# The address that an empty record reads in a gather: row 0 for all, or one row for each partition

## The reference, cut to what matters

```
support  = einsum(layernorm(x), W_weight) + W_bias         # 6250 x 256
messages = support[dst] * edge_weight[:, None]
x        = x + segment_sum(messages, src, 6250)
x        = x + lstm_part(layernorm(x))                      # 50 steps for 125 segments
```

## Time and profile before

| | us |
|---|---|
| median of 3 runs | 1850.2 |
| lowest, highest | 1849.69, 1853.89 |
| the profiled execution's own time | 1853.58 |
| its span | 1851.8 |
| busy: TensorE, VectorE, GpSimd, ScalarE | 1388.0, 1365.8, 1204.2, 543.2 |
| mean granted TensorE clock (share of full speed) | 0.885 |

### The profile page before, as it was taken

One profiled execution on the slowest core, in us unless ns is written; L12 is line 12 of the kernel. 1 busy time (PEld: TensorE's weight loads), 2 busy tenths in 40 slices (PEclk: granted clock), 3 DMA queues, 4 the chain that ended last, 5 costly groups with the idle time before them and its releaser, 6 DMA issues.

```text
span 1851.8 us, 34357 instructions
## 1 busy us (share of the span) xinstructions
PE 1388.0 (75%) x8625; PEld 1154.8 (62%) x8625; DVE 1365.8 (74%) x4146; ACT 543.2 (29%) x1869; POOL 1204.2 (65%) x1275
## 2 busy tenths in 40 slices
PE   5587744554555458998988888889889878999991
PEld 2345533443444333787777777777777668899991
DVE  7979778888888955677777777777777644566665
ACT  1112200000000000333333333333333346666660
POOL 0304867777777757777777777777777700477772
PEclk9778967777777775899999999999999999999995
DMA  8101343333333643444444444444444763333334
GB/s 210 26 23 35 50 137 76 79 79 74 80 79 74 77 61 106 128 137 141 144 138 138 139 137 139 139 136 139 138 137 137 109 124 114 113 113 112 113 101 139
DMA packets 77430, 202.26 MB, mean 109 GB/s; under 512 B 28529, under 2 KB 30790, under 8 KB 76392
## 3 DMA queue, kind: packets, MB, share of 16 engines
q0 software_dynamic: 53808, 116.85, 27.3%
q1 hardware_dynamic: 23584, 84.98, 14.2%
HBM read 160.49 MB, written 41.10 MB: 109 GB/s over the span
## 4 chain that ended last, share of the span: by engine, by line
PE 27%; POOL 24%; DVE 22%; issue 17%; DVEq 3%; DMA 3%; ACT 3%; SPq 0%; POOLq 0%; ACTq 0%
POOL big_a L522 22%; PE bank L1565 10%; DVE big_a L975 7%; PE bank L1485 5%; PE bank L1539 5%; PE bank L1514 4%; PE bank L1558 1%; DVEq L1049 1%; DVE big_c L1166 1%; ACT big_c L669 1%; DVE big_c L1171 1%; DVE listed L914 1%; ACT bank L662 1%; DVE stats L893 1%; PE bank L1433 1%
## 5 line engine op out<-in xcount | busy, mean ns | idle before, releaser
L522 POOL DMA_INDIRECT big_a<-support_scratch,stg_g x636 | 608.3, 956 | 207.0 <-issue 192.3
L1539 PE MATMUL bank<-big_a,big_c 128*125 128x256 f32 x1272 | 412.3, 416 | 92.0 <-issue 51.0
L1565 PE MATMUL bank<-big_c 128*128 128x125 f32 x3648 | 457.2, 277 | 26.9 <-DVE big_c L1171 23.8
L1565 PEld LDWEIGHTS bank<-big_c 128*128 128x128 f32 x3648 | 446.7, 192 | 48.7 <-issue 36.0
L1046 DVE TENSOR_TENSOR big_b<-big_b,bank 125x256 f32 x881 | 366.5, 416 | 132.0 <-PE bank L1539 82.9
L1040 DVE TENSOR_SCALAR big_c<-consts_sb,listed 128x125 f32<-128x125 f32 x881 | 318.8, 362 | 73.4 <-PE bank L1539 62.1
L1539 PEld LDWEIGHTS bank<-big_a,big_c 128*125 128x125 f32 x1272 | 202.7, 197 | 179.2 <-DVE big_c L1040 113.1
L492 POOL DMA_INDIRECT big_a<-support_scratch,stg_g x245 | 236.2, 964 | 82.2 <-issue 69.2
L1485 PE MATMUL bank<-big_a 125*128 125x192 bf16 x800 | 119.5, 332 | 214.1 <-DVE big_a L975 214.1
L1485 PEld LDWEIGHTS bank<-big_a 125*128 125x128 bf16 x800 | 100.4, 132 | 237.5 <-DVE big_a L975 229.4
L1558 PEld LDWEIGHTS bank<-xt,w_ih 128*128 128x128 f32 x1600 | 213.3, 195 | 13.8 <-ACT xt L578 1.9
(11 more groups left out here) (226 smaller groups left out, 1658.4 us busy)
## 6 DMA issues: line engine op xcount, KB each, us to landing
pr<-gate_input_scratch SPq DMA_DIRECT2D x64, 508.0 KB, 3.4
gate_input_scratch<-pr SPq DMA_DIRECT2D x50, 508.0 KB
big_a<-support_scratch,stg_g POOLq DMA_INDIRECT x881, 2.8
out<-big_a SPq DMA_DIRECT2D x5, 1120.0 KB
support_scratch<-pr SPq DMA_DIRECT2D x12, 448.0 KB
big_b<-in_x SPq DMA_DIRECT2D x2, 1904.0 KB
big_b<-in_x SPq DMA_DIRECT2D x1, 1792.0 KB
w_ih<-in_w_ih SPq DMA_DIRECT2D x1, 1024.0 KB
```

What stands on the lines that cost most here:

```text
L522: pool.indirect_dma_start(out=ring[:, s, :], out_offset=None, in_=sup_d, in_offset=bass.IndirectOffsetOnAxis(ap=stg_g[:, q, n:n + 1], axis ...
L1539: mm(bank[4 + s % PSR][0:SEGS, 0:D], oneh[:, s % HOTS, 0:SEGS], ring[:, s, :], start=True, stop=True).then_inc(prod, 1)
L1565: return mm(bank[b + x][:, c * SEGS:(c + 1) * SEGS], w_hh[:, k, g:g + P], h_s[:, q, k, :], start=False, stop=True, skip_group_check=True)
```

## The change

It adds one [128, 1] constant, `own_row`: the partition's number times 48 (N // P), so 0, 48, ..., 6096. In `unpack`, the cast of the unpacked rows to floats is replaced by two operations. The first writes `own_row` where the weight is zero and 0 elsewhere; the second takes the larger of that and the unpacked row. Empty records so read row 48 p in partition p. Descriptors, bytes and the destination of every gather are as they were.

```
+        own_row = sb("row_of_empty_records", [P, 1])
...
             link(V.tensor_scalar(block_no[:, 0:1], sums[:, 0:1], -1.0, float(P - 1), ALU.mult, ALU.add))
             split = float(PORTIONS[0])
+            V.tensor_scalar(own_row[:], block_no[:, 0:1], float(N // P), None, ALU.mult)
...
                 link(V.tensor_scalar(pack_i[:, 0:T], pack_i[:, 0:T], 7, None, ALU.arith_shift_right))
-                V.tensor_copy(row_of[:, a:a + T], pack_i[:, 0:T]).then_inc(unpacked, 1)
+                link(V.tensor_scalar(row_of[:, a:a + T], w_of[:, a:a + T], 0.0, own_row[:], ALU.is_equal, ALU.mult))
+                V.tensor_tensor(row_of[:, a:a + T], row_of[:, a:a + T], pack_i[:, 0:T], ALU.max).then_inc(unpacked, 1)
```

## The result

The changed kernel takes 1840.1 us (median of six runs, 1837.8 to 1843.8), the kernel before 1851.2 (six runs, 1849.7 to 1853.9). The ratio is 0.9934, with a 95% interval of 0.9922 to 0.9946: faster by 0.5 to 0.8%. The profiled execution took 1841.3 us (span 1839.5), against 1853.6 (1851.8): 12.3 us less.

The account below looks back on a forecast made before the run. GpSimd's gather issue paces portion two; in its tail, empty tiles all reading row 0 back up the DMA engines. Tail -14.9 plus operations +1.7 gives -13.2 us, from 1850.2 to 1837.0; own range 1833 to 1841, whole range 1832 to 1843.

Parts of the forecast that it names:

- The tail of portion two: Last, wholly empty tiles of portion two: with own rows no DMA backlog forms, saving 19.40 - 4.46 = 14.94 us.
- the last half's 4.46 us: End of portion two: the last half's final copy comes 4.46 us after its last gather's start, as in steady halves.
- The own rows: Gathers of empty tiles: reading 128 different rows costs the DMA engines 0.48 us a tile, like steady gathers.
- the lower of the two ends: DMA price of an own-row tile: 0.48 us from steady gathers, chosen over 1.60 us from same-row gathers.
- The first two rivals: Empty-tile gathers: own rows still cost 1.60 us (1851.9 us, chance 0.06), or between 1.256 and 1.60 (1844.4, chance 0.06).
- the one that made the kernel slower: Portion two's tail: 128 distant rows cost more than 1.60 us a tile; 1868.7 us at 2.2; chance 0.03.
- Portion one: Empty tiles ending portion one: their gather backlog hides under other work, such as VectorE's 14.10 us periods; saving nothing.
- Padding in filled tiles: 5216 empty slots in 822 filled tiles: taken as 0, at most 5.7 us; rival of more gain, 1831.3 us, chance 0.05.
- The added operations: Compare and maximum replacing the cast in unpack: 1.18 us in portion two plus 0.55 in portion one, 1.7 us lost.
- The maximum: Second added operation in unpack: 0.82 us for portion two's 636 columns, 0.40 for portion one's 245.
- The compare: First added operation in unpack: 0.81 us in portion two and 0.40 in portion one, scaled from a two-scalar operation.
- keeping the last halves near 20 us: Portion two's end, sign of a wrong prediction: gathers land early but TensorE or VectorE alone keeps last halves near 20 us.

Follow-up runs that it names:

- e3: Kernel before, with compare, maximum and own rows only in portion two's last 60 columns; ratio 1.0005 on a chip where the kernel before takes about 2380 us.
- e5: The kernel of e3 run again, against the kernel before, which took 2381.7 us on that chip; ratio 1.0009.
- e9: Shortened program ending when portion two is added, without recurrence or what follows; added operations kept, empty records read row 0; 1523.6 us.
- e10: The shortened program of e9 with one constant different, so that empty records read the change's own rows; 1514.2 us.
- e2: Changed kernel with own_row multiplied by 0, so empty records read row 0 with all added operations kept; ratio 1.0014 to the kernel before, about 2380 us there.
- e6: The kernel of e2 run again, against the kernel before, which took 2381.7 us on that chip; ratio 1.0006.
- e7: Changed kernel, but all empty records of a tile read one row, 9 times the tile's number; 2388.2 us, where the kernel before took 2381.7.
- e12: The shortened program of e9, but all empty records of a tile read one row, another in each tile, as in e7; 1515.6 us.
- e11: The shortened program of e9, but all empty records of all tiles read row 3000; 1527.0 us.
- e8: Changed kernel, but empty records in partition p read row 768 (p mod 8), eight rows in all; 2384.8 us, where the kernel before took 2381.7.

## Why the prediction was right

**The tail of portion two** was the right place, with the right mechanism: a tile at 0.46 us is hidden under GpSimd's issue, one at 1.60 is not. The forecast of 14.94 us came out as 14.07. The term that was mis-sized is the last half's 4.46 us, which measured 5.33. I took a steady half as the model. TensorE stands 1.43 us before a tile at 1491.46 us. The store at 1486.54 is no difference, since a steady half has one at nearly the same place: 2.96 us before its last gather (at 1440.89), and 2.71 here. What a steady half doesn't have is the first load of gate inputs, at 1489.63. The two gathers before the last one land in 3.7 us each here, the last two of the steady half in 2.8, though an earlier one of that half took 3.7 as well. That the load is the cause wasn't tried.

The median came to 1840.1 us where 1837.0 was forecast, 3.1 us more. The two terms, tail and operations, account for 0.6 of it, and 1.0 is that the kernel before has a median of 1851.2 over six runs and had 1850.2 over three. The other 1.5 are not explained; the six runs of the changed kernel spread over 6 us.

**The own rows** cost 0.46 us a tile; the lower of the two ends was the right choice. The first two rivals, own rows as slow as row 0 or partly so, are out by that number, and so is the one that made the kernel slower.

**Portion one** gave nothing, as forecast. VectorE's long operation in the changed kernel:

```profile
490.61 4.15 DVE L977 TENSOR_TENSOR big_a<-big_a,bank 125x3840 bf16<-125x3840 bf16 x1
...
505.26 4.14 DVE L977 TENSOR_TENSOR big_a<-big_a,bank 125x3840 bf16<-125x3840 bf16 x1
...
603.26 4.15 DVE L977 TENSOR_TENSOR big_a<-big_a,bank 125x3840 bf16<-125x3840 bf16 x1
...
617.91 4.14 DVE L977 TENSOR_TENSOR big_a<-big_a,bank 125x3840 bf16<-125x3840 bf16 x1
```

Two periods, full tiles and empty ones, are both 14.65 us. In both kernels the periods run through a cycle of eight, from 13.6 to 14.8 us; the earlier trace rows shows its place with 14.10, and this is the one with 14.65. Portion one's gathers take 416.1 us from first to last, where they took 415.8.

**Padding in filled tiles** gave nothing either: from its first gather to its last portion two takes 800.4 us, and took 800.8. e3 and e5 were to show it directly and couldn't, on chips where nothing was to be gained. e9 and e10 do show it, in the shortened program and with one constant between them: 795.4 and 795.1 us for portion two, 416.2 and 416.6 for portion one.

**The added operations** were put at 1.7 us and measure 1.43. The maximum was right, 0.82 and 0.42 against 0.82 and 0.40. The compare was wrong, 0.55 and 0.35 against 0.81 and 0.40: the row I scaled it from, L1151, has two scalars per partition, and this one has an immediate and one. The Trainium skill ("VectorE: DVE Perf Modes", "The perf-mode tier table") has tensor_scalar in fp32 at double rate. The trace agrees here: 0.55 and 0.35 us, beside 0.49 and 0.29 for the cast. The price by itself is shown only by durations; e2 and e6, at 1.0014 and 1.0006, agree with it and can't narrow it.

**What the prediction lacked** is a condition, and it is the larger lesson. It named TensorE as what could take the gain, by keeping the last halves near 20 us, but gave that no chance, since the rows of before spoke against it. On two of the three chips of the experiments that is how the kernel ran: halves of 24 us, and a gain of nothing. The forecast holds for chips of the first kind only; had the result come from one of the second, it would have been wrong. The rows of before, all from one execution, couldn't tell that there is a second. The whole program with own rows was timed on a chip of the first kind in the result alone. Why TensorE's matmuls come late on the others stays open; the profile says no more than "issue".

## What to carry to other kernels

Where padding gathers real memory, don't let all of it read one address: look at the busy share and the GB/s of the DMA engines together, because a high share at a low rate (here 0.95 at 75 GB/s, where 0.47 gave 137) means that the same bytes have become dearer. The slow gather cost something only where it was slower than the engine that issues gathers and the one that uses them, so price the tail tile by tile against both. And time a change on more than one chip: this one was worth 11 us on a chip of the first kind and nothing on one of the second. A cheaper form of this change would do the compare on the last columns alone (e3). In e3's trace it lengthens portion two's unpacking by 0.39 us, where the full form costs 1.43, so by estimate it saves 1 us more; it ran only where no gain was to be had, so that is not shown.

## What the hardware showed that I had not expected

- One row read by all 128 descriptors of a gather cost 0.64 to 0.74 us of the DMA engines when the next gather read another row (e7, e12), and 1.25 to 1.65 when it read the same again (e2, e6, e9, e11). I had taken the meeting within one gather to be the whole of it. What in the memory makes the difference wasn't tried.
- Eight rows, each read 16 times in a gather and again in the next, were as cheap as 128 different ones: 0.45 (e8) against 0.44 to 0.46 us.
- The same kernel took 1850 to 1855 us on some chips and 2374 to 2387 on two others, over 58 runs there.
